# A decoder layer on one core: an own order for the last steps, x1 plus the cross attention's bias row in a buffer of its own, and the second norm applied by ScalarE

## The reference

```python
x = x + nystrom_attention(layernorm(x))              # 16 heads of 16, 64 landmarks,
                                                     # pseudo-inverse by 6 Newton iterations
x = x + cross_attention(layernorm(x), ctx, ctx, mask)  # 64 keys an item
x = x + expert_ffn(layernorm(x))                     # one of 8 experts per item, chosen
                                                     # from the last token
```

```python
for _ in range(6):
    KV = x @ V
    V = 0.25 * V @ (13.0 * I - KV @ (15.0 * I - KV @ (7.0 * I - KV)))
```

## Time and profile before

| | |
|---|---|
| median of three runs | 1508.6 us (1506.45 to 1513.19) |
| the profiled execution's own time | 1512.32 us |
| its span in the profile | 1510.3 us |
| mean granted PE clock, share of full speed | 0.983 |
| PE busy | 1435.8 us, 95% |
| DVE busy | 1014.2 us, 67% |
| ACT busy | 744.4 us, 49% |
| POOL busy | 569.5 us, 38% |

### The profile page before, as it was taken

The page is one execution under the profiler, slowest core; times in us unless marked ns, Lnnn a source line. Parts: engine busy times, 40 slices in busy tenths (PEclk is TensorE's granted clock), DMA queues, the critical chain, the costliest instruction groups (busy, mean ns, idle before and its releaser), DMA issues.

```text
span 1510.3 us, 51059 instructions
## 1 busy us (share of the span) xinstructions
PE 1435.8 (95%) x22484; PEld 947.6 (63%) x22484; DVE 1014.2 (67%) x2098; ACT 744.4 (49%) x1434; POOL 569.5 (38%) x688
## 2 busy tenths in 40 slices
...
DMA packets 40270, 53.02 MB, mean 35 GB/s; under 512 B 9442, under 2 KB 30194, under 8 KB 40050
## 3 DMA queue, kind: packets, MB, share of 16 engines
...
## 4 chain that ended last, share of the span: by engine, by line
PE 89%; issue 6%; DVE 2%; POOL 2%; ACT 1%; POOLq 1%; DMA 0%; SPq 0%; DVEq 0%; ACTq 0%
PE bank L1051 41%; PE bank L1069 7%; PE bank L1276 7%; PE bank L1079 6%; PE bank L1263 4%; PE bank L1163 3%; PE bank L1122 3%; PE bank L1231 2%; PE bank L1143 2%; PE bank L1172 2%; PE bank L1059 2%; PE bank L1244 2%; PE bank L1149 1%; PE bank L1222 1%; PE bank L1157 1%
## 5 line engine op out<-in xcount | busy, mean ns | idle before, releaser
L543 POOL TENSOR_TENSOR b<-ut,eye 128x256 f32<-128x256 f32 x192 | 136.8, 731 | 361.3 <-DVE ut L896 341.7
L701 ACT ACTIVATE az<-bank 128x320 f32<-128x320 f32 x192 | 66.7, 399 | 200.5 <-PE bank L1069 200.0
L1051 PE MATMUL bank<-xnT_c,w1e 128*128 128x512 f32 x256 | 129.5, 632 | 8.8 <-DMA row_e<-w2o_row 8.8
L952 DVE RECIPROCAL oT_x<-bank 128x256 f32<-128x256 f32 x64 | 107.7, 1724 | 35.2 <-PE bank L1276 35.2
L649 ACT ACTIVATE p<-bank,nm 128x512 f32<-128x512 f32 x128 | 87.0, 688 | 83.2 <-DVE nm L841 83.0
L1051 PE MATMUL bank<-xnT_a,wqkv 128*128 128x512 f32 x256 | 125.5, 614 | 0.0
L1051 PE MATMUL bank<-w2e,hT 128*128 128x256 f32 x512 | 118.8, 385 | 2.7 <-ACT hT L756 2.7
L719 ACT ACTIVATE pT<-bank 128x512 f32<-128x512 f32 x128 | 69.5, 604 | 104.8 <-PE bank L1265 104.7
L952 DVE RECIPROCAL oT<-bank 128x256 f32<-128x256 f32 x64 | 112.4, 1756 | 6.8 <-PE bank L1276 4.3
L926 DVE TENSOR_REDUCE m<-bank 128x8 f32<-128x512 f32 x128 | 82.2, 684 | 46.4 <-PE bank L1231 46.4
L447 POOL TENSOR_SCALAR var_eps_c<-mv_c 128x4 f32<-128x4 f32 x16 | 3.7, 234 | 283.0 <-DVE mv_c L777 283.0
...
## 6 DMA issues: line engine op xcount, KB each, us to landing
...
```

Source lines behind the costliest of these rows:

```text
L543: return g.tensor_tensor(b7[:, q, :], ut[:, q, :], eye[28 if it else 7][:].unsqueeze(1) .broadcast_to([P, 4, LM]), ALU.subtract).then_inc( ...
L952: return v.reciprocal(oT[x][:, k, half], tile(i, ("den" + x, k))[:, half]).then_inc(dve_done, 1)
L1051: last = mm(dst, lhsT, rhs, start=(k == 0), stop=(k == len(pairs) - 1))
```

## The change

`LAST` is a list of 514 steps with their item numbers, for items 12 to 15. `program()` leaves these steps out of the turns and appends them in the order of the list. `TURN` is written anew as well: the steps that run once are placed otherwise, and a few neighbours change places. The step `nmB` on ACT is new: it applies the second norm as nmC does the third, from a shift that POOL's lnB now forms. `x1b` writes into a new buffer `x1_box`, and wx adds that one.

```diff
-    S.fc A.az.4.0-11 D.lmq.0-10 A.az.4.1-11 A.e1.1.2-11 P.den1.0-11 D.wb.4.0-11 D.wb.4.1-11 D.lmq.1-10
...
+    S.fc D.uz.4.0-3 P.fb P.s2-2 G.b7.5.0-3 D.rec1.1.0-3 P.iZ.5-3 A.az.5.0-3 G.b7.5.1-3 P.iT.5-3
...
+    A.f.2-1 P.p3T.2-2 A.h.0-4 A.p3T.3-2 A.p3T.2-2 P.x2T-2 G.xr-2 S.f.3-2 A.x2T-2 P.s3.1-2 A.p3T.1-2
+    G.lnB-3 A.nmB-3 A.f.7-2 D.mx3.1.3-2 P.a.0-2 D.mx3.1.2-2 P.a.1-2 P.f.2 A.e3.1.3-2 P.zT.0-2
+    D.mx3.1.0-2 P.y3.1-4 S.x-1 P.xnTb.0-3 A.e3.1.0-2 G.kbd-2 S.w2.0-1 S.w2.6-1 P.xnTb.1-3 D.fb-1
+    A.zT.0-2 P.p3T.7-2 D.mx3.1.1-2 A.e3.1.1-2 A.e3.1.2-2 P.p3T.4-2 A.xnTb.0-3 P.f.5-2 A.xnTb.1-3
...
+LAST = """
+    A.az.0.1@14 D.y3.0@12 A.xnTa.1@15 P.jT.0@14 D.mx1.1.1@14 S.out@12 P.jZ.0@14 D.ut.0.1@14 P.xnTa.0@15
...
+    A.ex.1.0@14 G.kxbd@15 P.logit@13 D.uz.5.0@15 P.ox.0@14 A.ex.1.3@14 D.uz.5.1@15 D.rec1.1.1@15
+    A.ex.1.2@14 P.y@15 A.ex.1.1@14 P.denx.0@14 D.logit@13 D.y@15 P.denx.1@14 S.exp@13 D.recx.0.0@14
+    P.o1.0@15 P.o1.1@15 D.recx.1.0@14 P.ox.1@14 D.o1.0@15 P.vx@15 D.o1.1@15 D.recx.0.1@14 P.w1.1@15
+    D.recx.1.1@14 P.w1.0@15 D.w1.1@15 G.row@13 P.h.2@13 D.w1.0@15 D.ox.1@14 D.lnB@15 P.h.0@13 A.h.2@13
+    P.h.3@13 D.ox.0@14 A.h.0@13 G.lnB@15 D.vx@15 P.wx.1@14 A.h.3@13 A.nmB@15 P.wx.0@14 D.wx.1@14
+    P.xnTb.1@15 D.wx.0@14 P.xnTb.0@15 A.xnTb.1@15 P.h.1@13 D.lnC@14 G.x1b@15 A.xnTb.0@15 P.qx.1@15
+    A.h.1@13 G.rsC@14 P.qx.0@15 A.qx.1@15 A.nmC@14 P.sx.1@15 P.y3.1@13 D.mxx.1.0@15 A.qx.0@15
+    D.mxx.1.1@15 D.mxx.1.3@15 D.mxx.1.2@15 P.sx.0@15 D.y3.1@13 P.y3.0@13 D.mxx.0.2@15 D.mxx.0.0@15
+    D.mxx.0.3@15 D.mxx.0.1@15 D.mpx@15 P.xnTc.1@14 P.xnTc.0@14 D.y3.0@13 A.xnTc.1@14 P.mTx@15
+    A.xnTc.0@14 S.out@13 A.mTx@15 P.gate@14 P.tx.0@15 A.gate@14 P.tx.1@15 A.ex.0.2@15 A.ex.0.1@15
+    P.logit@14 A.ex.1.1@15 D.logit@14 A.ex.1.2@15 G.base@14 S.exp@14 A.ex.0.3@15 A.ex.0.0@15 A.ex.1.0@15
+    P.denx.0@15 A.ex.1.3@15 P.ox.0@15 D.recx.0.0@15 P.denx.1@15 P.ox.1@15 D.recx.1.0@15 D.recx.0.1@15
+    D.recx.1.1@15 P.h.3@14 G.row@14 D.ox.0@15 P.h.2@14 D.ox.1@15 A.h.3@14 P.wx.0@15 A.h.2@14 P.wx.1@15
+    D.wx.0@15 P.h.0@14 D.wx.1@15 D.lnC@15 P.h.1@14 A.h.0@14 G.rsC@15 A.h.1@14 P.y3.1@14 A.nmC@15
+    P.xnTc.1@15 D.y3.1@14 P.xnTc.0@15 A.xnTc.1@15 P.y3.0@14 A.xnTc.0@15 P.gate@15 D.y3.0@14 A.gate@15
+    S.out@14 P.logit@15 D.logit@15 S.exp@15 G.base@15 P.h.2@15 G.row@15 P.h.1@15 A.h.2@15 P.h.3@15
+    A.h.1@15 P.h.0@15 A.h.3@15 A.h.0@15 P.y3.0@15 P.y3.1@15 D.y3.0@15 D.y3.1@15 S.out@15
 """

+LAST_STEPS = [(parse(w)[0], int(i), parse(w)[1]) for w, i in (word.split("@") for word in LAST.split())]

-    steps = []
+    steps, last = [], set(LAST_STEPS)
     for turn in range(BATCH + DEPTH):
         for engine, step, back in TURN_STEPS:
             i = turn - back
             if 0 <= i < BATCH and not (i and once(step)):
-                steps.append((engine, i, step))
-    return steps
+                if (engine, i, step) not in last:
+                    steps.append((engine, i, step))
+    return steps + LAST_STEPS

+        shift_b = sb("shift_b", [P, T])
+        x1_box = sb("x1_box", [P, T, D])

                 if kind == "lnB":
                     if c := unmet(pool, "D", i, ("lnB",)):
                         pool.wait_ge(dve_done, c)
+                    if c := unmet(pool, "A", i - 1, ("nmB",)):
+                        pool.wait_ge(act_done, c)
                     layer_rstd("b")
-                    if c := unmet(pool, "P", i - 1, ("xnTb", 0), ("xnTb", 1)):
-                        pool.wait_ge(pe_done, c)
-                    return normalise("b", x1).then_inc(pool_done, 1)
+                    g.tensor_tensor(shift_b[:], mv["b"][:, :, 0], rstd["b"][:], ALU.mult)
+                    g.drain()
+                    return g.tensor_scalar(shift_b[:], shift_b[:], -1.0, None, ALU.mult).then_inc(pool_done, 1)
                 if kind == "x1b":
                     if c := unmet(pool, "D", i, ("lnB",)):
                         pool.wait_ge(dve_done, c)
-                    if c := unmet(pool, "G", i, ("lnB",)):
-                        pool.wait_ge(pool_done, c)
+                    if c := unmet(pool, "D", i - 1, ("wx", 0), ("wx", 1)):
+                        pool.wait_ge(dve_done, c)
                     all_consts(pool)
-                    return add_row(x1[:], x1[:], box_row).then_inc(pool_done, 1)
+                    return add_row(x1_box[:], x1[:], box_row).then_inc(pool_done, 1)

+                if kind == "nmB":
+                    if c := unmet(act, "D", i, ("w1", 0), ("w1", 1)):
+                        act.wait_ge(dve_done, c)
+                    if c := unmet(act, "G", i, ("lnB",)):
+                        act.wait_ge(pool_done, c)
+                    if c := unmet(act, "P", i - 1, ("xnTb", 0), ("xnTb", 1)):
+                        act.wait_ge(pe_done, c)
+                    for t in range(T):
+                        last = s.activation(xn["b"][:, t, :], x1[:, t, :], ACT.Identity, bias=shift_b[:, t:t + 1],
+                                            scale=rstd["b"][:, t:t + 1])
+                    return last.then_inc(act_done, 1)

-                    dst, res = (x1, xr) if kind == "w1" else (x2, x1)
+                    dst, res = (x1, xr) if kind == "w1" else (x2, x1_box)
                     if kind == "w1":
                         if c := unmet(dve, "G", i, ("xr",)):
                             dve.wait_ge(pool_done, c)
-                        if c := unmet(dve, "D", i - 1, ("wx", 0), ("wx", 1)):
-                            dve.wait_ge(dve_done, c)
+                        if c := unmet(dve, "G", i - 1, ("lnB",), ("x1b",)):
+                            dve.wait_ge(pool_done, c)
+                        if c := unmet(dve, "A", i - 1, ("nmB",)):
+                            dve.wait_ge(act_done, c)

-                    if x == "c":
-                        if c := unmet(pe, "A", i, ("nmC",)):
+                    if x in "bc":
+                        if c := unmet(pe, "A", i, ("nmC",) if x == "c" else ("nmB",)):
                             pe.wait_ge(act_done, c)
```

More of the change, by code:

```diff
@@ L35 @@
[L35 to L44, removed]
@@ L50 @@
[L50 to L54, removed]
@@ new lines @@
+    A.az.5.1-3 D.wb.5.0-3 S.exp-4 P.h.2-4 D.wb.5.1-3 P.f.1-1 A.h.2-4 D.s2-2 P.jZ.5-3 P.h.1-4 D.uz.5.1-3
+    D.uz.5.0-3 D.rec1.1.1-3 A.f.3-1 S.f.0-2 S.f.5-3 S.w2.2 P.y-3 P.s3.0-2 D.y-3 P.o1.0-3 P.o1.1-3
+    D.rec1.0.1-3 D.mx3.0.1-2 D.o1.0-3 P.h.3-4 P.f.7-2 D.o1.1-3 S.f.6-3 D.mx3.0.0-2 G.row-4 D.mx3.0.3-2
+    A.e2-2 A.e3.0.1-2 A.e3.0.0-2 P.w1.1-3 P.w1.0-3 D.mx3.0.2-2 A.e3.0.3-2 P.p3T.0-2 A.e3.0.2-2 D.soft2-2
+    A.h.3-4 D.w1.1-3 P.p3T.3-2 P.h.0-4 D.w1.0-3 S.f.1-2 A.h.1-4 A.p3T.0-2 P.p3T.1-2 D.lnB-3 S.f.2-2
@@ new lines @@
+    A.f.2-1 P.p3T.2-2 A.h.0-4 A.p3T.3-2 A.p3T.2-2 P.x2T-2 G.xr-2 S.f.3-2 A.x2T-2 P.s3.1-2 A.p3T.1-2
+    G.lnB-3 A.nmB-3 A.f.7-2 D.mx3.1.3-2 P.a.0-2 D.mx3.1.2-2 P.a.1-2 P.f.2 A.e3.1.3-2 P.zT.0-2
+    D.mx3.1.0-2 P.y3.1-4 S.x-1 P.xnTb.0-3 A.e3.1.0-2 G.kbd-2 S.w2.0-1 S.w2.6-1 P.xnTb.1-3 D.fb-1
+    A.zT.0-2 P.p3T.7-2 D.mx3.1.1-2 A.e3.1.1-2 A.e3.1.2-2 P.p3T.4-2 A.xnTb.0-3 P.f.5-2 A.xnTb.1-3
+    P.p3T.5-2 A.a.1-2 D.lnA-1 P.p3T.6-2 P.qx.0-3 A.a.0-2 A.p3T.4-2 G.cst-2 A.p3T.7-2 P.s1.0-2 A.p3T.5-2
+    A.p3T.6-2 A.f.5-2 D.y3.1-4 P.zT.1-2 D.mx1.0.1-2 G.b7.0.1-2 P.kx.0-2 G.b7.0.0-2 D.mx1.0.2-2 P.f.0-1
@@ new lines @@
+    D.mx1.1.1-2 P.k.0-1 P.iZ.1-2 P.iT.1-2 A.k.0-1 D.mx1.1.3-2 P.kx.1-2 D.mx1.1.2-2 S.w2.3 D.mx1.1.0-2
+    D.wb.1.0-2 P.tx.0-3 A.az.1.0-2 D.wb.1.1-2 A.az.1.1-2 A.ex.0.0-3 A.ex.0.2-3 P.jT.1-2 D.ut.1.0-2
+    P.jZ.1-2 D.ut.1.1-2 A.ex.0.1-3 A.ex.0.3-3 P.f.3 D.mp1-2 D.uz.1.1-2 P.tx.1-3 A.ex.1.0-3 G.b7.2.1-2
+    A.ex.1.1-3 A.ex.1.3-3 P.denx.0-3 A.ex.1.2-3 P.k.1-1 D.uz.1.0-2 D.recx.0.0-3 G.b7.2.0-2 D.recx.0.1-3
+    P.mT1-2 P.denx.1-3 D.recx.1.0-3 P.ox.1-3 P.ox.0-3 A.k.1-1 A.mT1-2 G.x1b-3 S.f.7-3 D.ox.0-3 P.vx-2
```

73 lines of the change are left out of this document (58 added, 15 removed).

## The result

Times are medians. The changed kernel takes 1496.5 us (1494.9 to 1498.9, 8 runs), the kernel before 1508.6 (1503.8 to 1518.4, 8 runs): ratio 0.9914, 95% interval 0.989 to 0.9938, so 12 us (9 to 17) faster. Forecast were 1481 us and 27.5 us. The value lies in the range of 1464 to 1502 by luck: that range was made wide by other terms, and what happened doesn't stand among the rivals.

What follows compares the result with a forecast made beforehand. PE work was taken to bound the middle, so only the ends could give: 26 us from the last part plus 1.5 from the start, off 1512.3, less 3.7 for the profiled execution, gave 1481 us; range 1464 to 1502.

Steps and rivals of the forecast that it cites:

- (a): Last steps, from jT.0 of item 14: reordering fills PE's idle time; with the last item's norm, 26 us gained.
- The clock assumption: Last part: filler keeps PE's clock up except behind the wait for the expert's DMA; otherwise 12 us longer.
- 6.8 + 4.3: Ahead of item 15's w1: 6.8 us because DVE bounds, 4.3 for waits in six Newton rounds.
- (b): Second norm moved from POOL to ACT: 2.5 us saved on the last item, 0 in a steady turn.
- a longer change of table: Rival, chance 0.04: ACT needs 1.4 us more before e3, so each turn loses 0.6 us; 1489 us.
- nmB in ACT's queue: Slower rival, chance 0.09: the norm's 2.07 us and a 1.28 us table load lie open each turn; 1531 us.
- (c): x1 in its own buffer: 0, between -0.5 and +2.4 us in all.
- (d): Steady turn and start: turn unchanged, banks emptied early but for tx.1; 1.5 us gained at the start.
- a turn over 87.5: Sign in the steady loop that the forecast is wrong; 86.5 to 87.2 us was expected.
- PE's busy share from 171 to 1279 us: Sign in the middle of the span: the share was to stay at 99%.
- The term of 1.5 us for the start: Start, 84 to 171 us: 1.5 of PE's 7.2 us idle saved, between -4 and +3.

Runs made afterwards that it cites:

- oldturn_norm: The kernel before with the second norm on ACT and x1_box, in the old turn and without the list LAST: 1506.7 us, ratio 1.0005.
- mp_early: The changed kernel with one step of the turn moved, D.mp1 before D.ut.1.0 instead of behind D.ut.1.1: 1472.9 us, ratio 0.9765.
- oldturn_last: The changed kernel with the old order of the turn, keeping the list LAST, x1_box and the norm on ACT: 1483.6 us, ratio 0.9839.

## Why the prediction was wrong, point by point

- **(a) The list LAST: right in its sum, not in each term.** Forecast: w1 of item 15 starts 110 us after jT.0 of item 14, and the end lies 95 behind it. Measured: 1403.18 - 1291.85 = 111.3 and 1497.2 - 1403.18 = 94.0. The part takes 205.35 us against 231.0, a gain of 25.6 where 26 stood. Windows of the last part, PE clock in the third column from the right:

```profile
1291.85:1420.00 128.15, 120.36 (x2241) 77.29 (x2238) 98.34 (x196) 61.09 (x124) 37.75 (x51) 0.97 0.05 16
1420.00:1497.20 77.20, 57.42 (x308) 36.45 (x306) 22.08 (x42) 21.24 (x35) 11.68 (x11) 0.91 0.15 52
```

  Its last stretch is at 0.91 where the earlier trace rows has 0.79, with 8.8 us for row_e's DMA and 2.8 for ACT's pT_x as the large waits left. The clock assumption held in part only. In this part PE is granted half clock (0.50) three times: for 10.2 us from 1470.7 on, within the wait for the expert's DMA and the h behind it, as assumed; but also for 3.4 us from 1440.0 on, behind the wait for pT_x, and for 6.8 us from 1375.1 on, ahead of w1, where the forecast had none. The same matmuls at half clock and at full clock:

```profile
1380.45 0.68 PE L1345 MATMUL bank<-mT,minus 32*128 32x512 bf16 x4
...
1385.25 0.42 PE L1345 MATMUL bank<-mT,minus 32*128 32x512 bf16 x4
...
1438.82 1.06 PE L1356 MATMUL bank<-pT_x,ones_bd 128*32 128x512 f32 x8 [2.78 <-ACT pT_x L787]
...
1441.09 2.01 PE L1356 MATMUL bank<-pT_x,ones_bd 128*32 128x512 f32 x8
```

  Ahead of w1 PE was idle for 7.8 us, not for the 11 that stood as 6.8 + 4.3; and 103.5 us were busy where 98.9 of work stood, which the slow clock explains in part. That the 110 came out so well is partly luck.
- **(b) The norm on ACT: right.** Nothing in a turn waits for ACT; oldturn_norm is level with before. The rivals "a longer change of table" and "nmB in ACT's queue" fall. Where ACT loads its table in the changed kernel it takes 1.28 us with the next ACTIVATE 1.29 to 1.30 behind it (986.34 to 987.63, 996.06 to 997.36), as in the earlier trace rows; the drain of 1.38 that the Trainium skill adds ("ScalarE: Activation LUTs", What ACT_TABLE_LOAD costs) is not seen.
- **(c) x1_box: 0 in a turn, but not idle.** In LAST the w1 of item 15 stands before the wx of item 14. With one buffer w1 would overwrite what that wx still reads. The order that brings the 25.6 us needs this part.
- **(d) The turn: the step that failed.** "The bank handed to each step was emptied early but for tx.1". q.0's is not: D.ox.0 empties it, 0.86 us late in each turn. But a bank list would not have shown the cause. The step looked at PE's steps and took every DVE duration over from the rows of before. The new order moves D.mp1 behind ut.1 and G.x1b behind b7.2, and there the two are beside each other: 2.9 us more on DVE a turn. By the experiments this costs PE 1.85 us a turn (88.2 against 86.3 in the same order without the clash). The profiled execution of before has a turn of 87.4 and not 86.3, so over the twelve turns between the rows above 14.0 us show, where the forecast had 0. Both signs that the prediction had named for this show it: "a turn over 87.5" is what happened, and PE's busy share from 171 to 1279 us fell to 1082.0 of 1108.0, 98%, where 99% was forecast. The term of 1.5 us for the start isn't settled: y3.0 of item 0 comes 2.0 us sooner, but among the four kernels with the old turn it comes anywhere from 225.6 to 229.1 us.
- **The rivals.** The slower one looked for the cost of a turn in ACT's queue, because the change puts new work there. It lay with the two engines whose work the change only reorders.
- **The order by itself is good.** Without the clash the new turn is 86.3 us. Against the old turn's undisturbed 86.75 that is 0.45 less, and mp_early lies 10.7 us under oldturn_last; 13 turns of 0.45 are 6 of these. I had costed it at nothing.

Open: of the 1.85 us a turn the waits show 1.36; the rest lies in PE's busy time, whose ends are modelled. What in the new order makes the undisturbed turn shorter was not taken apart. Single turns of the old order are longer in some executions (90.08 us once in the profiled one of before, where the new order with mp1 early has 86.2 to 86.6); no run was made on that.
